# One-core decoder layer with top-2 experts: the first nine expert tiles listed from batches 0 to 5 and run ahead of the second gate group

## Time and profile before

| | us |
|---|---|
| three runs: median (lowest, highest) | 758.21 (753.84, 759.27) |
| the profiled execution | 758.85 |
| its span, first to last instruction | 756.9 |
| PE busy in the span | 625.6 |
| VectorE, ScalarE, POOL busy | 512.5, 383.8, 318.7 |

### The profile page before, as it was taken

The page is one execution under the profiler, slowest core; times in us unless marked ns, Lnnn a source line. Parts: engine busy times, 40 slices in busy tenths (PEclk is TensorE's granted clock), DMA queues, the critical chain, the costliest instruction groups (busy, mean ns, idle before and its releaser), DMA issues.

```text
span 756.9 us, 22821 instructions
## 1 busy us (share of the span) xinstructions
PE 625.6 (83%) x8056; PEld 454.8 (60%) x8057; DVE 512.5 (68%) x1110; ACT 383.8 (51%) x799; POOL 318.7 (42%) x277
## 2 busy tenths in 40 slices
PE   2676787999999999998986677379999999999940
PEld 1444665676666666665653445267777777777730
DVE  5685777876775877756676768836666666666635
ACT  4333575667657575575868451134444444444414
POOL 2886154544444356211101049424444454444422
PEclk9777899999999999999999799679999999999985
DMA  8243442141240302312253121202232222322226
GB/s 251 79 136 99 140 140 79 50 118 40 62 124 12 88 16 71 93 49 76 82 158 123 58 84 31 110 29 43 42 48 49 42 42 42 54 43 42 43 29 220
DMA packets 39831, 59.33 MB, mean 78 GB/s; under 512 B 6768, under 2 KB 27504, under 8 KB 39632
## 3 DMA queue, kind: packets, MB, share of 16 engines
q1 hardware_dynamic: 32272, 48.12, 21.6%
q0 software_dynamic: 7488, 10.23, 8.4%
HBM read 34.08 MB, written 11.67 MB: 60 GB/s over the span
## 4 chain that ended last, share of the span: by engine, by line
PE 63%; DVE 14%; DMA 6%; ACT 6%; issue 5%; POOL 2%; SPq 2%; ACTq 0%; DVEq 0%; POOLq 0%
PE bank L1580 8%; PE bank L1195 5%; DVE mxc L962 5%; PE bank L1582 4%; PE bank L1221 4%; PE exp_scores L1246 3%; PE bank L1570 3%; ACT probs L710 3%; PE bank L1174 3%; PE max_scores L1266 2%; PE max_scores L1570 2%; PE exp_scores L1260 2%; PE bank L1176 2%; PE bank L1175 2%; PE bank L1572 2%
## 5 line engine op out<-in xcount | busy, mean ns | idle before, releaser
L710 ACT ACTIVATE probs<-exp_scores 128x768 f32<-128x768 f32 (+1 forms) x128 | 117.5, 918 | 107.0 <-PE exp_scores L1252 53.3
L616 POOL DMA_INDIRECT acc_rows<-x_res,slot_row x39 | 65.4, 1677 | 122.1 <-DVE x_res L1119 119.1
L1580 PE MATMUL bank<-w_sb,wp 128*128 x312 | 110.0, 380 | 2.0 <-DVE wp L1106 2.0
L962 DVE TENSOR_REDUCE mxc<-max_scores 128x4 f32<-128x1024 f32 x64 | 78.2, 1221 | 39.9 <-PE max_scores L1266 39.8
L1582 PE MATMUL bank<-w_sb,wp 128*128 x312 | 85.0, 273 | 0.0
L927 DVE TENSOR_REDUCE mx<-max_scores 128x6 f32<-128x768 f32 x64 | 60.9, 952 | 30.8 <-PE max_scores L1234 30.6
L777 ACT ACTIVATE probs<-bank,b_sb 128x128 f32<-128x128 f32 x152 | 43.5, 370 | 65.6 <-PE bank L1572 65.6
L1104 DVE CAST wp<-probs 128x512 f16<-128x512 f32 x78 | 33.9, 434 | 62.6 <-ACT probs L777 62.6
L777 ACT ACTIVATE probs<-max_scores,b_sb 128x128 f32<-128x128 f32 x160 | 45.6, 369 | 58.1 <-PE max_scores L1572 58.0
L1195 PE MATMUL bank<-probs,w_sb 128*32 128x256 f32 x768 | 56.3, 396 | 9.6 <-ACT probs L710 8.8
L1570 PE MATMUL max_scores<-xT,w_sb 128*128 128x128 f16 x320 | 60.7, 223 | 1.2 <-DVE xT L1098 1.2
(11 more groups left out here) (230 smaller groups left out, 1726.0 us busy)
## 6 DMA issues: line engine op xcount, KB each, us to landing
w_sb<-w_sb SPq DMA_DIRECT2D x192, 64.0 KB, 2.2
wstage<-in_w_exp SPq DMA_DIRECT2D x16, 512.0 KB, 4.1
w_sb<-in_w_exp SPq DMA_DIRECT2D x8, 512.0 KB, 4.6
wp<-in_w_exp SPq DMA_DIRECT2D x8, 512.0 KB, 4.0
x_sb<-in_x_by_feature SPq DMA_DIRECT2D x8, 256.0 KB, 3.4
ctx_raw<-in_ctx SPq DMA_DIRECT2D x8, 256.0 KB, 3.6
x_res<-in_x SPq DMA_DIRECT2D x8, 256.0 KB, 3.6
x_rows<-x SPq DMA_DIRECT2D x8, 256.0 KB, 2.4
```

The lines of the kernel that those rows point to most:

```text
L616: nc.gpsimd.indirect_dma_start(out=acc_rows[:, :], out_offset=bass.IndirectOffsetOnAxis(ap=slot_row[:, n:n + 1], axis=0), in_=yb[n % 2], i ...
L710: nc.scalar.activation(probs[:, 2 * (k % 2):2 * (k % 2) + 2, 0:cols], ps_e[:, :, 0:cols], ACT.Exp, scale=(SELF_SCALE, CROSS_SCALE)[a]).the ...
L962: nc.vector.tensor_reduce(mxc[:, 2 * k:2 * k + 2, :], ps_m[:, :, :].rearrange("p h (a k) -> p h a k", a=2), axis=AX.X, op=ALU.max).then_in ...
L1580: mm(o[:, 0:2 * D], ah[:, u, f, :], weights(e, at, 2 * D), start=(f == 0), stop=(f == FC - 1), skip_group_check=True)
```

## The change

The two groups stay, but the first alone now lists nine tiles. gate_first_tiles takes from the counts of batches 0 to 5 the full tiles of each expert, in order of experts until nine are had; gate_first_table and gate_first_rows make slot_row and slot_w for these nine, and POOL (gather_first) gathers the first two of them in its order. The second group has no words in the orders: its steps stand between the tiles. All other tiles, 30 of them, are listed from all tokens less the nine. `gate_weights` moves from POOL to ScalarE: VectorE makes plain one-hots, two operations of 256 columns per token tile, and ScalarE scales them by token number and by weight, three operations. The table of slots of the first group is added up after each four scatters in bank 2. The stores of x2 have two semaphores, up to batch 5 and after. Slots of all tiles use bank 0, the second group's products bank 1. kv_transpose moves to bank 2, self_negate to bank 0, cross_back and cross_out to bank 1. The gate's scratch is in x_res and ctx_raw, yb in x1. Tiles 0 to 8 are written out, the loop has 14 iterations instead of 17. All five orders are new; their ends and beginnings:

```diff
 TENSOR_ORDER (end)
-...ce2.7 cw.6 ce3.7 gr.5 cv1.7 ce4.7 ce5.7 cv2.7 ce6.7 x2.6 ce7.7 lg.6 cv3.7 gs0.5 co.7
-gs1.5 cb.7 gs2.5 cw.7 gs3.5 gs4.5 x2.7 lg.7 gs5.5 gr.7 gs0.7 gs1.7
+cn.7 ce0.7 ce1.7 cv0.7 ce2.7 ce3.7 gr.5 ce4.7 cv1.7 cb.6 ce5.7 cv2.7 ce6.7 gs0.5 ce7.7 cw.6 cv3.7 gs1.5 co.7 cb.7
+gs2.5 x2.6 lg.6 gs3.5 cw.7 gs4.5 gs5.5 gf.5 x2.7 lg.7
 SCALAR_ORDER (start, end)
+xt.0 ph0.0 wh0.0 wh1.0 sq.0 ph1.0 xt.1 qc.0 ph2.0 cx.0 ...
+... cb.6 ce5.7 gw0.5 wh2.6 ce6.7 cv1.7 cv2.7 ce7.7 gw1.5
+cv3.7 gw2.5 cb.7 wh3.6 wh0.7 x2.6 gw3.5 gw4.5 wh1.7 wh2.7 gw5.5 wh3.7 x2.7
 VECTOR_ORDER (end)
-wl3.6 gh0.5 cs.6 gh1.5 lg.6 co.7 gh2.5 gh3.5 gh4.5 cw.7 cl.7 cs.7 gh5.5 wl0.7 wl1.7 lg.7 g1.7 gS.5 g2.7 g3.7 gc.7 gh0.7
-gh1.7 wl2.7 wl3.7 gS.7
+g2.5 g3.5 gh0.5 ge.5 gh1.5 gS0.5 cw.6
+wl1.6 wl2.6 gS1.5 gh2.5 co.7 cl.6 cs.6 gh3.5 gS2.5 wl3.6 wl0.7 gh4.5 cw.7 gS3.5 cl.7 cs.7 gh5.5 wl1.7 gS4.5 lg.6 wl2.7
+gS5.5 gR.5 lg.7 wl3.7
 GPSIMD_ORDER (end)
-cx.7 cr.5 sr.7 ss.7 cr.6 gw0.5 ke.7 gw1.5 gw2.5 gw3.5 gw4.5 cr.7 gw5.5 gw0.7 gw1.7
+cr.5 cx.7 sr.7 ss.7 ke.7 cr.6 cr.7 gg.5
 SYNC_ORDER (start, end)
-w0.0 rl0.0 rl1.0 x.0 w1.0 rl2.0 rl3.0 x.1 w2.0 rl4.0 c.0 ...
+x.0 rl0.0 w0.0 w1.0 rl1.0 c.0 r.0 rl2.0 rl3.0 x.1 w2.0 rl4.0 ...
+w2.6 s.5 w3.6 w0.7 w1.7 s.6 w2.7 s.7 w3.7
```

```diff
-GATE = {5: (0, 0, 12), 7: (1, 12, 16)}
+SEEN, FIRST = 6, 9
+GATE = [(0, 0, SEEN * TT), (1, SEEN * TT, NT)]
...
+            def gate_values(t):
+                act_e.wait_ge(v_oh, t + 1)
+                nc.scalar.activation(oh_vals[:, t % 2, :, 0, :], oh_row[:, t % 2, :, :], ACT.Identity,
+                                     scale=tab[:, C_TOK1 + t:C_TOK1 + t + 1])
+                for c in range(2):
+                    last = nc.scalar.activation(oh_vals[:, t % 2, c, 1, :], oh_row[:, t % 2, c, :], ACT.Identity,
+                                                scale=rs1[:, 4 + c, t:t + 1])
+                last.then_inc(a_oh, 1)
...
+            def gate_onehots(t):
+                if t >= 2:
+                    dve.wait_ge(pe_slot, 2 * (t - 1))
+                lanes = tab[:, C_LANE:C_LANE + P].unsqueeze(1).broadcast_to([P, 2, P])
+                for o, i in ((oh_lane, 2), (oh_row, 0)):
+                    last = nc.vector.tensor_tensor(o[:, t % 2, :, :], lanes,
+                                                   rs1[:, i:i + 2, t].unsqueeze(2).broadcast_to([P, 2, P]), ALU.is_equal)
+                last.then_inc(v_oh, 1)
...
+                elif u == "gather_first":
+                    pool.wait_ge(v_rows, 1)
+                    pool.wait_ge(x2_st[0], 32 * SEEN)
+                    pool.wait_ge(z_st, 32)
+                    gather(0)
+                    gather(1)
...
             AHEAD = 4
-            for n in range(AHEAD):
+            pool.wait_ge(x2_st[1], 32 * (B - SEEN))
+            for n in range(2, AHEAD):
                 gather(n)
             for n in range(N_TILES):
+                if n + AHEAD - 1 == FIRST:
+                    pool.wait_ge(v_rows, 2)
```

VectorE, ScalarE and PE in the expert stage:

```diff
+            dve.wait_ge(v_lg, B)
+            gate_shift(*GATE[1])
+            dve.wait_ge(v_te, 1)
+            dve.wait_ge(v_rows, 1)
+            low_slots(0, 0)
+            gate_choose(*GATE[1])
+            low_slots(1, 1)
             dve.wait_ge(b2_ld, 16)
...
+            for n in range(FIRST):
+                tile(n, n % 2, n > 0)
+                if n:
+                    weigh(n - 1, (n - 1) % 2, 16 * (n - 2) if n > 2 else None)
+                if n == 0:
+                    gate_slots(*GATE[1])
+                elif n in (1, 2):
+                    gate_onehots(GATE[1][1] + 2 * (n - 1))
+                    gate_onehots(GATE[1][1] + 2 * (n - 1) + 1)
+                elif n == 3:
+                    gate_late_tiles()
+                elif n == 4:
+                    dve.wait_ge(pe_slot, 2 * NT)
+                    nc.vector.tensor_tensor(slots_all, ps_slots[1], slots_kept, ALU.add).then_inc(v_S, 1)
+                elif n == 5:
+                    gate_late_rows()
...
+            for n in range(FIRST):
+                tile(n, n % 2, 2 * (n - 1) if n >= 2 else None, n > 0)
+                if n in (2, 3):
+                    gate_values(GATE[1][1] + 2 * (n - 2))
+                    gate_values(GATE[1][1] + 2 * (n - 2) + 1)
...
-            pe.wait_ge(v_S, 2)
-            pe.wait_ge(v_sel, 1)
...
+            pe.wait_ge(v_lg, B)
             pe.wait_ge(v_rows, 1)
...
+                if n == 0:
+                    gate_ranks(*GATE[1])
+                elif n in (2, 3):
+                    for t in range(GATE[1][1] + 2 * (n - 2), GATE[1][1] + 2 * (n - 1)):
+                        gate_scatter(1, t, GATE[1][1], NT - 1)
+                elif n == 5:
+                    gate_table(1, slots_all, FIRST, N_TILES)
```

More of the change, by code:

```diff
@@ L93 @@
[L93 to L102, removed]
@@ L310, in decoder_layer @@
         m_b = sb("m_b", [P, NT, E], BF16)
-        ex = [sb(f"ex{i}", [P, E]) for i in range(4)]
+        ex = [sb(f"ex{i}", [P, E]) for i in range(5)]
+        own, wide, pick = ex[4], kvn[:, :, :].rearrange("p t k -> p (t k)"), sq[:, 0:2 * E]
         slot_w = sb("slot_w", [P, N_TILES])
@@ L327, in decoder_layer @@
         al = wp[:, 2 * FC * P:4 * FC * P].rearrange("p (u f t) -> p u f t", u=2, f=FC)
-        yb = [x_res[:, i, :] for i in range(2)]
+        yb = [x1[:, i, :] for i in range(2)]
         fin = w_sb[:, 0:NT * D * 2].bitcast(F32).rearrange("p (t d) -> p t d", d=D)
@@ L395, in decoder_layer @@
         pe_xc, a_xc = sem("pe_stacks_transposed"), sem("stacks_ready")
-        v_x2, x2_st = sem("x2_ready"), sem("x2_stored")
+        v_x2 = sem("x2_ready")
+        x2_st = [sem(f"x2_stored{i}") for i in range(2)]
         pe_x2T, a_x2T = sem("pe_x2_transposed"), sem("x2T_ready")
@@ L530, in _, with gather @@
             nc.gpsimd.memset(c_sb[:, :, :, :], 1.0).then_inc(c_ms, 1)
+            def gather(n):
+                if n >= 2:
+                    pool.wait_ge(pe_ft, n - 1)
+                nc.gpsimd.indirect_dma_start(
+                    out=xg[n % 2], out_offset=None, in_=x2_rows[0:SEEN * T, :] if n < FIRST else x2_rows[:, :],
+                    in_offset=bass.IndirectOffsetOnAxis(ap=slot_row[:, n:n + 1], axis=0)).then_inc(g_ld[n % 2], 16)
             def inverse_root(value, have, n, done):
@@ L1297, in bank1_free @@
             def bank1_free():
+                once(a_n2[1], at["cross_back"])
                 once(v_n1[1], at["cross_norm"])
+                once(v_r[1], at["cross_out"])
                 once(a_o[1], at["cross_pv0"])
-                once(v_kvT, at["kv_transpose"])
+                once(v_rows, at["gate_first"])
                 once(v_qc, at["latents"])
@@ L1309, in bank2_free @@
                 once(v_key, at["gate_ranks"])
-                once(v_sel, at["gate_ranks"] - 1)
-                once(v_mT[0], at["self_negate"])
+                once(v_S, at["gate_scatter"])
+                once(v_kvT, at["kv_transpose"])
                 once(v_n1[0], at["self_norm"])
@@ L1317, in bank3_free @@
                 once(v_ct, at["content1"])
-                once(a_n2[1], at["cross_back"])
-                once(v_r[1], at["cross_out"])
                 once(v_lg, at["logits"])
@@ L1523, in _ @@
[L1523 to L1534 removed]
+                    gate_ranks(*GATE[0])
@@ L1543, in _ @@
                     at[u] = b + 1
-            pe.wait_ge(v_S, 2)
-            pe.wait_ge(v_sel, 1)
-            for i in range(2):
-                last = mm(bank[0][:, i * N_TILES:(i + 1) * N_TILES], slots_all[:, i * P:(i + 1) * P], slot_t[2][:, :], start=True, stop=True)
-            last.then_inc(pe_fin, 1)
+            pe.wait_ge(v_lg, B)
             pe.wait_ge(v_rows, 1)
```

534 lines of the change are left out of this document (280 added, 254 removed), and 3 rows, old and new, of the table UNITS.

## The result

| | before | after |
|---|---|---|
| median of the runs (lowest, highest), us | 756.75 (752.14, 762.95) | 751.03 (747.34, 758.63) |
| the profiled execution | 758.85 | 748.55 |
| its last transpose of cross maxima (end of the attention stage) | 428.88 | 418.87 |
| its first product of tile 0 | 496.52 | 480.43 |

The ratio is 0.9926, 95% interval 0.9902 to 0.9951: 5.7 us faster, in the range 742 to 763 (and in the narrower 748 to 757) and 2 us under the forecast of 753. By medians the change brought 5.7 us where 6.0 were forecast.

A forecast was written before the change was run, and what follows sets the result against it. The prediction took PE to bound the 39 expert tiles at 5.87 us each, after a 25 us handover mostly filled by VectorE. It summed 758.85 - 11.5 + 7.0 - 1.5 = 752.85, forecast 753 us, range 742 to 763 (own range 748 to 757).

The forecast's parts named there:

- Part 3: New orders and banks: first rope product at 16.3 us instead of 17.8, -1.5 us; the rest 0, with 5 either way.
- Part 1: Handover: tile 0 no longer waits for the second gate group, starting at 485 (bounds 479 to 492), 11.5 us earlier.
- Part 2: Expert stage: the second gate group's steps inserted between tiles add 7.0 us on saturated PE.
- no gain from it: Ahead of tile 0: PE again waits over 5 us, so the low clock stays as before, 0.61; no gain.
- the ranks: After tile 0: ten tiny PE products for the second group's ranks add 0.4 us.
- the wait for the low slots of tile 2: gate_slots after tile 0's splits delays tile 2's low slots on VectorE; PE waits 0.7 us.
- a round of scatters: After tiles 2 and 3: two token tiles each, PE waits and scatters, 2.7 us a round, 5.4 for both.
- the scalings: ScalarE's scalings of late one-hots after tiles 2 and 3: 1.2 us per token tile.
- 0 taken, 2 as a bound: gate_late_tiles, 17 small VectorE operations beside tile 4, delays tile 5's low slots; counted as 0 us, at most 2.
- Within 5 us of before: End of the attention stage: its last product was to come at most 5 us from its old time.
- The good case: Better handover: VectorE's waits vanish, tile 0 starts at 479, late group costs 2.8 us; 743 us, chance 0.25.
- Slower rounds: First group's six scatter rounds each cost more; at 2.5 us more, tile 0 starts at 500, total 768; chance 0.12.

The follow-up runs named there:

- values_early: Changed kernel, but ScalarE scales the late one-hots between the two halves of a tile's hidden layer instead of behind them; 750.06 us, ratio 0.9913.
- best2: Changed kernel with handover, late-scaling and start words moved, the late-tile list cut in two, and VectorE's slot additions earlier; 742.81 us, ratio 0.9816.
- orders_new: Kernel before with the changed kernel's bank moves and orders up to the last cross maxima, old gate kept; 755.46 us, ratio 0.9986.
- orders_again: Second profiled execution of the kernel before with new orders and banks but the old gate; profiled at 754.31 us.

## Why the prediction was right

**The whole.** The forecast was 758.85 - 11.5 + 7.0 - 1.5. By medians on one chip Part 3 alone (orders and banks) brought 756.21 - 755.46 = 0.8 us of its 1.5, and Parts 1 and 2 on top of it 4.9 where 4.5 were forecast; the 0.8 is within noise, the 4.9 is not. Along the time axis the terms are less right, and that the total fits is in part luck. By the means of three profiled executions of the changed kernel and two of before the last maxima come 9.4 us earlier (427.9 to 418.4), where only Part 3's 1.5 was allowed ahead of the handover. The handover shrinks by 5.3 us (67.9 to 62.6), where Part 1 had 11.5. The two errors nearly cancel: tile 0 starts 14.8 us earlier, forecast 13.0. The insertions are 7.0, as forecast.

**Part 1, tile 0 at 485 and held by the last weight piece.** It started at 480.43, 478.36 and 484.30 in three executions, one of them 0.6 us outside the stated 479 to 492, always held by the last low part. The step that failed is the stretch behind the attention stage. My 485 came from rows of before with the stage's end left where it was, so it allowed 485 - 428.88 = 56.1 us; it took 61.2 to 65.1. Two things were missed. The working never followed SP's queue, where the new order puts the store of x2 of batch 6 behind a load that waits; it cost VectorE 2.99 us. And the sentence on the clock ("no gain from it") went by the stretch 472 to 497 alone: over the whole stretch the clock is lower with the changed orders, 0.66 to 0.72 in the three executions against 0.80 and 0.82 before. What made up for it is that the attention stage ended 9.4 us earlier.

**Part 2, insertions 7.0.** From tile 0 to the end of the span the three executions of the changed kernel take 266.2, 267.5 and 268.1 us, the two of before 260.4 and 260.2: 5.8 to 7.9, 7.0 by the means. To the slot transposes of tile 5 it is 32.04 - 25.57 = 6.5 us in the first pair, just the 0.4 + 0.7 + 5.4 of the sum. The five tiles behind it, four of them written out, then give 1.15 back (28.65 us, where the same five in the loop of before took 29.80), and the gather of tile 11 takes some of that again; no term had either. Within the 6.5 the ranks are 0.4, as forecast; the wait for the low slots of tile 2 is 1.01 (0.7); a round of scatters 0.67 + 2.11 = 2.8 and 0.81 + 2.11 = 2.9 (2.7), with PE waiting once before both token tiles rather than before each; the scalings 0.98 us a token tile (1.2). The Trainium skill, ScalarE: Activation LUTs, section What ACT_TABLE_LOAD costs, was used wrongly there: these scalings have one pointer operand, not two, and an estimate by its figures is 0.40 for an activation of 256 columns and 0.29 for one of 128 in sequence, 0.98 a token tile. The trace agrees. The term "0 taken, 2 as a bound" for the list of late tiles proved hidden only by another wait: once ScalarE's was removed, the list cost PE the same 2 us (values_early). It has 16 operations in the trace, not 17.

**Part 3, -1.5, and 0 for the rest.** The latents came as worked out, at 7.40 instead of 12.30, but the first rope product at 18.59 and not at 16.3, 1 us later than before (17.62): the 1.5 us were not had there. What it did not see is that the words behind it fill better, so that the first two batches gain 12 to 15 us; and that with the old gate words most of this is lost again up to tile 0. "Within 5 us of before" was wrong for the last product of the attention stage (8 to 12, from pair to pair), yet the orders alone are worth next to nothing in the end. Why the lead melts wasn't settled; the stretch before the last maxima shows a part of it.

**The rivals.** The good case (743) was reached, but only by best2. Slower rounds were seen in part: the last two of the six scatter words had waits of 3.14 and 2.32 us ahead of them.

## What to carry to other kernels

When work is moved ahead, walk each queue of the order past the new place, stores above all: a word that waits holds a store behind it, and a buffer that the store reads holds an engine. When a wait is taken away, name the engine that is late next and cut its list before counting the gain: 2 us on ScalarE only showed 2 us on VectorE. And compare like executions: two profiled executions of one kernel lay up to 7 us apart at the same step (tile 0 of orders_new and orders_again, 498.20 and 491.08), so a step's gain is to be taken from several, or from medians of kernels that differ in that step alone.

## What was not expected of the hardware

- The granted clock in a stretch of small, waiting products differs between executions of the same words, 0.66 to 0.76, and the stretch is 5 us shorter at the higher. Products in PE's waits whose results nobody reads raised it from 0.78 to 0.95 at the same busy time of PE. The Trainium skill, TensorE: Matmul & The Clock Gate, section Why this matters for your kernels, advises to keep TensorE busy against a fall of its clock; these runs agree, also for products whose results aren't used.
- A cast of 128 columns on VectorE took 1.19 us while POOL was in two operations, and the next one, from another tile, 0.21 after them (VectorE, then POOL, at the start of the changed kernel):

```profile
28.89 1.19 DVE L981 CAST ident_h<-tab 128x128 f16<-128x128 f32 x1
30.00 0.21 DVE L982 CAST mask_b<-probs 128x128 bf16<-128x128 f32 x1
```

```profile
27.72 2.27 POOL L577 TENSOR_TENSOR w_sb<-w_sb 128x512 f16<-128x512 f32 x2
```

The Trainium skill, SBUF — State Buffer, section Who interferes with whom, says that one pair of ports is shared by VectorE and GpSimd and locked for a whole instruction. These rows agree; no run tested it.
